# A transformer stack on one core: one maximum unit moved ahead of each score step, and another order of preparation in the 32-wide self-attention

## The reference

```python
x = x + _L0_xattn_ref(_layernorm(x), ctx_512, ...)   # causal self-attention + attention to the context, 16 heads of 8
x = x + _L0_ffn_ref(...)
x = x + _L1_xattn_ref(_layernorm(x), ctx_512, ...)   # attention to the context, 16 heads of 8
x = x + _L1_ffn_ref(...)
x = x + _L2_xattn_ref(_layernorm(x), ctx_512, ...)   # 16 heads of 32: self-attention (mask after softmax), MLP, then context, MLP
x = x + _L2_ffn_ref(...)
x = x + _L3_xattn_ref(_layernorm(x), ctx_512, ...)   # attention to the context, 16 heads of 8
x = x + _L3_ffn_ref(...)

# inside _L2_xattn_ref, the first _mha
a = softmax(einsum('bhsd,bhtd->bhst', q, k) * D ** (-0.5))
a = a * (t <= s)
o = einsum('bhst,bhtd->bhsd', a, v)
```

## Time and profile before

| what | value |
|---|---|
| median of 3 runs | 8038.86 us (8022.59 to 8043.93) |
| the profiled execution | 8022.59 us, its span 8020.8 us |
| PE busy | 7135.1 us, 89% |
| DVE busy | 5918.4 us, 74% |
| ACT busy | 4951.6 us, 62% |
| POOL busy | 2313.2 us, 29% |
| TensorE clock granted, mean | 0.94 of full speed |

### The profile page before, as it was taken

How to read it: one execution, slowest core, us unless ns; L and a number is a source line. 1 busy time by engine, 2 the same in 40 slices (tenths; PEclk the granted TensorE clock), 3 DMA queues, 4 the chain that set the end, 5 groups by cost and what they waited for, 6 DMA issues and landing times. The chain is left out here.

```text
span 8020.8 us, 186125 instructions
## 1 busy us (share of the span) xinstructions
PE 7135.1 (89%) x73814; PEld 3142.3 (39%) x73814; DVE 5918.4 (74%) x12885; ACT 4951.6 (62%) x9846; POOL 2313.2 (29%) x2368
## 2 busy tenths in 40 slices
PE   6999999878999997888599999999998779999979
PEld 2333333353333333444244444444444533333335
DVE  6888888657989996677466666666665469899855
ACT  4778887636888884444255555555554248888852
POOL 1222222111121110444245444544444211221200
PEclk9999999888999998788699999999999779999989
DMA  4444333114433421000100000000000144434400
GB/s 97 101 95 92 83 83 92 45 26 100 99 89 77 99 65 31 15 16 13 53 6 8 7 6 10 6 10 6 7 3 18 49 83 96 96 84 85 97 22 14
DMA packets 319828, 417.80 MB, mean 52 GB/s; under 512 B 56533, under 2 KB 238053, under 8 KB 318968
## 3 DMA queue, kind: packets, MB, share of 16 engines
q1 hardware_dynamic: 317432, 405.36, 22.4%
q10 hardware_dynamic: 1536, 0.53, 0.0%
HBM read 225.41 MB, written 174.66 MB: 50 GB/s over the span
## 5 line engine op out<-in xcount | busy, mean ns | idle before, releaser
L687 ACT ACTIVATE a_probs<-scores_ps 128x512 f32<-128x512 f32 (+2 forms) x5248 | 2821.7, 591 | 356.2 <-PE scores_ps L607 263.4
L746 DVE TENSOR_REDUCE a_unit_max<-bank 128x1 f32<-128x512 f32 x3072 | 2004.0, 684 | 182.0 <-PE bank L594 147.3
L624 PE MATMUL bank<-a_probs,a_v_sb 128*9 128x256 f32 (+1 forms) x20992 | 1614.1, 379 | 29.4 <-ACT a_out_sb L694 20.4
L1275 ACT ACTIVATE cross_probs<-scores_ps 128x512 f32<-128x512 f32 (+1 forms) x1792 | 869.4, 571 | 772.6 <-PE scores_ps L1172 772.6
L1357 DVE TENSOR_REDUCE cross_unit_max<-bank 128x1 f32<-128x512 f32 x1536 | 1006.5, 687 | 319.7 <-PE bank L1158 316.9
L607 PE MATMUL scores_ps<-a_stack 64*128 64x256 bf16 (+1 forms) x10496 | 1131.5, 275 | 61.6 <-ACT a_probs L687 55.8
L1441 POOL TENSOR_TENSOR cross_added<-cross_probs 128x1024 f32<-128x1024 f32 x384 | 902.4, 2350 | 944.6 <-PE bank L1205 868.8
L746 DVE TENSOR_REDUCE a_unit_max<-scores_ps 128x1 f32<-128x512 f32 x1536 | 1050.2, 684 | 162.1 <-PE scores_ps L594 144.6
L594 PE MATMUL bank<-a_stack 63*128 63x512 bf16 (+2 forms) x3413 | 1039.7, 372 | 8.1 <-DMA a_stack<-a_stack_dram 2.6
L607 PEld LDWEIGHTS scores_ps<-a_stack 64*128 64x128 bf16 (+1 forms) x10496 | 373.5, 96 | 991.9 <-ACT a_probs L687 832.8
L594 PE MATMUL scores_ps<-a_stack 63*128 63x512 bf16 (+2 forms) x1707 | 635.9, 373 | 50.8 <-DMA a_stack<-a_stack_dram 47.5
(11 more groups left out here) (421 smaller groups left out, 10119.5 us busy)
## 6 DMA issues: line engine op xcount, KB each, us to landing
a_stack_dram<-a_parts SPq DMA_DIRECT2D x288, 400.2 KB, 4.3
a_stack<-a_stack_dram SPq DMA_DIRECT2D x256, 348.2 KB, 8.0
a_stack<-a_stack_dram SPq DMA_DIRECT2D x128, 444.2 KB, 9.9
a_ctxT<-in_ctxT SPq DMA_DIRECT2D x48, 400.2 KB, 4.9
a_stack_dram<-a_parts SPq DMA_DIRECT2D x288, 64.0 KB, 2.7
a_stack_dram<-a_parts SPq DMA_DIRECT2D x96, 128.0 KB, 2.8
f_x<-x_after_dram SPq DMA_DIRECT2D x32, 256.0 KB, 3.6
x_after_dram<-a_res SPq DMA_DIRECT2D x48, 128.0 KB, 4.6
```

Source lines behind the costliest of these rows:

```text
L624: ins = pe.matmul(out_bank[32 * h:32 * h + V8, q0:TOK], v[0:n, e.t, 4 * e.g + h, :], A.probs[0:n, held, o + q0:o + TOK], start=(e.t == 0), ...
L687: act.activation(by_pair(A.probs[0:n, b, a * 512:(a + 1) * 512])[:, :, q0:TOK], by_pair(score_bank[(2 * e.i + a) % 3][0:n, :])[:, :, q0:TO ...
L746: ins = dve.tensor_reduce(unit_max[:, e.g % 2, qt, 2 * a + j, c:c + 1], bank[:, 0:e.s.chunks[c][1]], AX.X, ALU.max)
L1275: act.activation(probs[0:n, b, h, 0:m, :].rearrange("p m q -> p (m q)"), score_bank[h][0:n, 0:m * TOK], ACT.Exp, scale=scale).then_inc(S[" ...
```

## The change

In `segment8` the first unit of each step now stands before the step's scores instead of behind them; the second stays where it was. In `segment32`, for the self-attention only, the layer norms, the turned input and the first two `qk` and the first quad's units are made earlier in the list (for the batch after the next one), each `turn` belongs to the next batch, and the values move to steps 2 and 3. Third, DVE copies the values out of their bank instead of ACT.

```diff
@@ segment8
         units = units_at.get(n, [])
+        plan += units[0:1]
         if with_core and n < end:
             plan.append(Ev("scores", s=steps[n][0], g=steps[n][1], t=steps[n][2], i=cur * end + n))
-        plan += units[0:2]
+        plan += units[1:2]
         i = n - LAG8
@@ segment32
     if s.own:
         if with_ahead:
-            for i, kind in enumerate(("ln1", "ln2", "ln3", "ln4")):
-                put(i, 2, kind)
-        prepare(1, 1, True, "x_turned")
+            for i, slot, kind in ((0, 0, "ln1"), (0, 1, "ln2"), (1, 0, "ln3"), (1, 2, "ln4"), (2, 0, "x_turned"), (2, 2, "qk")):
+                put(i, slot, kind)
+            for k in range(s.NU):
+                units_at.setdefault(3, []).append(Ev("unit", k=k, r=int(k == s.NU - 1)))
+            put(3, 2, "qk", g=1)
         for g in range(QUADS):
-            step, late = (g + 1) % QUADS, g == QUADS - 1
-            prepare(step, 2, not late, "qk", g=g)
-            step, late = (g + 2) % QUADS, g >= QUADS - 2
-            for k in range(s.NU):
-                prepare(step, 0, not late, "unit", g=g, k=k, r=int(k == s.NU - 1))
-            prepare((g + 3) % QUADS, 0, g == 0, "turn", g=g)
-        prepare(3, 1, True, "v", j=0)
-        prepare(0, 1, False, "v", j=1)
+            if g >= 2:
+                prepare(g - 2, 2, True, "qk", g=g)
+            for k in range(s.NU * (g > 0)):
+                prepare(g - 1, 0, True, "unit", g=g, k=k, r=int(k == s.NU - 1))
+            prepare(g, 0, True, "turn", g=g)
+        prepare(2, 1, True, "v", j=0)
+        prepare(3, 1, True, "v", j=1)
         proj_at = (2, 1)
@@ segment32, the batch of an event
-        if e.kind in AHEAD32 and not (s.own and e.kind == "x_turned"):
+        if e.kind in AHEAD32 or s.own and e.kind in ("qk", "unit") and not e.nxt:
             e.batch = cur + 2
@@ program_act: "v" of the self-attention is no longer its work
-                if e.kind in SIDE32 and e.kind != "proj" and not (own and e.kind == "turn"):
+                if e.kind in SIDE32 and e.kind != "proj" and not (own and e.kind in ("turn", "v")):
...
-                    if e.kind == "v" and own:
-                        ins = act.activation(v_sb[:, m, e.j, :], side_bank[:, :], ACT.Copy)
@@ program_dve
+                if e.kind == "v" and own:
+                    dve.wait_ge(S["side_ps"], e.n + 1)
+                    dve.tensor_copy(v_sb[:, p, e.j, :], side_bank[:, :]).then_inc(S["side_done"], 1)
```

More of the change, by code:

```diff
@@ L1302, in program_act @@
                         ins = act.activation(k_tiles(e, 0), side_bank[:, 0:n].rearrange("p (j n) -> p j n", n=P), ACT.Copy)
-                    if e.kind == "v" and own:
-                        ins = act.activation(v_sb[:, m, e.j, :], side_bank[:, :], ACT.Copy)
-                    if e.kind == "v" and not own:
+                    if e.kind == "v":
                         n = s.tiles[2 * e.j][1]
```

## The result

| kernel | median | range of runs |
|---|---|---|
| before | 8032.98 us (4 runs) | 8022.59 to 8043.93 |
| changed | 8227.05 us (4 runs) | 8218.04 to 8235.57 |

The ratio is 1.0242 [1.0222, 1.0261]: slower by some 194 us. The direction was forecast, and 8227 lies inside the range of 7960 to 8270, but the forecast was 8122 (its sum adds 96 us to the profiled execution of before), and its own range ended at 8190. What has to be explained is a rise twice as large as foreseen.

What follows compares the result with a forecast made beforehand. Attention was taken as paced by DVE (about 1.2 us a plain step) or ACT's loop (1.14), own by its step's chain; 8022.6 us + 48 (attention) + 48 (own) = 8119, stated as 8122, range 7960 to 8270 us.

Steps and rivals of the forecast that it cites:

- term of the stage own: Stage own: +2.0 us of chain and +1.0 us of clock a batch, 16 batches, +48 us, between -20 and +80.
- `turn` behind `x_turned`: Own, step 2: `turn` must wait for ACT's two copies behind the four exponentials, +2.0 us a batch.
- `proj` behind `v`: Own: `proj` stands behind a `v` and waits for its copy, now DVE's, +0.85 us a batch.
- `x_turned` and `ln2` leave, `ln2` before the reciprocal: Own: `x_turned` leaves step 1's chain, `ln2` its place before a `turn` copy, perhaps delaying the reciprocal 0.2: -0.85 us a batch.
- clock (PE busy): Own: about 3 us of idle PE in step 2 may lower the clock; a third of 3.1 us, +1.0 a batch.
- The attention term: Stages a0, a1, a3: the even unit ahead of the scores costs +1.0 us a batch, 48 batches, +48 us.
- behind four `turn`s and four `quad_out`s: Attention: ACT already waits there, so the next exponential starts 0.22 us later; half of 1.7 us counted, +0.8 a batch.
- DVE's earlier unit: Attention: DVE gets the even unit about 0.22 us earlier, -0.5 us a batch of at most -1.3.
- The faster one: Rival: the even unit fills PE's waits and feeds DVE earlier, -62 us, own +0: 7960 us; 22%.
- Nothing to be seen: Rival: attention gains and loses alike, own loses less than thought, within 24 us of before, 8000 to 8046; 18%.
- ACT's loop shows everywhere: Rival: DVE does not pace, plain steps take 1.225 us, full-array side jobs cost 0.21; attention +211, 8282 us; 12%.
- Strict order across the row halves: Rival: PE keeps program order, units no longer run in pairs, 7.7 us a batch, +370 us, with own 8440 us; 5%.

Runs made afterwards that it cites:

- e6: Changed kernel with segment8 as before, plus the first `v` of a batch moved to step 1 in own: 8109.57 us, ratio 1.0081 to before.
- e8: Changed kernel with segment8 as before, plus `ln2` at the end of step 0 and `ln3` in slot 1 of step 1: 8108.14 us, ratio 1.0081.
- e7: Changed kernel with segment8 as before, GpSimd adding one head of four in own, the other sums left out: 8113.33 us, ratio 1.0091.
- e5: Changed kernel with segment8 as before, plus `turn` put ahead of `x_turned` in step 2 of own: 8093.09 us, ratio 1.0061.
- e3: Kernel before with the segment8 edit alone and even units on rows 64 to 127, odd on 0 to 63: 8032.35 us, ratio 0.9996.
- e4: Kernel before with only the rows of the units swapped, both units still behind the scores: 8048.62 us, ratio 1.0011.
- e1: Kernel before with the segment8 edit alone: 8127.69 us, ratio 1.0114.
- e11: Changed kernel with segment8 as before, plus 16 unused small matmuls ahead of every `turn`'s wait in own: 8137.59 us, ratio 1.0145.
- e9: Changed kernel with segment8 as before, plus the edits of e5, e6 and e8 together: 8064.39 us, ratio 1.0051.
- e12: e3 plus 16 unused small matmuls ahead of every `turn`'s wait in own: 7998.93 us against 8025.1 before, ratio 0.9971.

## Why the prediction was right or wrong

**The step that failed is the term of the stage own**, "+3.0 us a batch, 16 batches: +48 us". It measured +115, outside its own bounds of -20 to +80. By its own parts, per batch over the ten batches:

| part | forecast | measured |
|---|---|---|
| `turn` behind `x_turned` | +2.0 | +1.9 |
| `proj` behind `v` | +0.85 | +0.78 |
| `x_turned` and `ln2` leave, `ln2` before the reciprocal; `ln3` and copy of `v` at 0 | -0.85 | +1.5 |
| PE idle, sum | +2.0 | +4.2 (6.0 to 10.2) |
| clock (PE busy) | +1.0 | +3.6 (29.5 to 33.1) |
| batch | +3.0 | +7.85 (35.5 to 43.3) |

The +1.9 is how much later `turn` starts behind the first exponential, the +0.78 a wait; the +1.5 is what the sum of idle time leaves beside the two. Counted as waits alone, PE's in the ten batches of before and of the changed kernel are, for each batch: `turn` for ACT's line 1321 0 and 2.5 us, `turn` for maxima 3.4 and 4.1, units 2.3 and 2.65, `proj` 0 and 0.78.

Three things went wrong.
- *The clock was sized at a third of its bound.* The bound, 3.1 us between a batch at 0.90 and one at 0.77, was itself too small. The same trace of before has batches, from one `x_turned` to the next, that lie further apart:

```profile
3433.40:3471.60 38.20, 33.98 (x303) 18.23 (x302) 26.33 (x58) 17.20 (x32) 17.00 (x19) 0.73 0.05 15
```

```profile
3680.40:3713.10 32.70, 25.25 (x303) 14.13 (x302) 26.09 (x58) 17.10 (x32) 16.98 (x19) 1.00 0.05 14
```

  They differ by 5.5 us in length and by 8.7 us of PE's busy time, for the same 303 matmuls. The low level, half of full speed, covers 22.5 us of a batch in the record of the clock now and 10.2 before. e6 and e8 show directly that here an edit worth little or nothing in idle time moves the stage by 33 us.
- *"`ln3` stays before a `turn` copy: 0."* It stayed before the copy, but in a step in which GpSimd's addition is still under way. What was checked was DVE's order, not what runs on GpSimd beside it. e7 shows this cause. That `ln2`, now before the reciprocal, was foreseen to cost 0.2 and costs more is only read in the trace: the `turn` behind it waits 2.31 us for its maximum, where 1.18 is usual. e8 moves both norms at once and does not part them.
- *The run-in was not in the sum.* An order that prepares two batches ahead has 24 us more to do before the first exponential, and the last batch gives 9 us back. "+3.0 us a batch, 16 batches" has no such term. The batches themselves, +6.7 us in each of the other 15, are still the larger part of the miss.

The parts hold one against another as well: the `turn` wait (e5) alone makes half of the loss, and its mechanism, place and size of 1.9 us are as forecast.

**The attention term, +48, measured +75.** The mechanism stood: e3 takes it away with the order untouched. Per step in a1 (from one exponential to the next, medians) plain steps alternate between 1.15 and 1.30 us, mean 1.22, as worked out; the mean was already 1.19 before. Steps behind a `turn` went from 1.41 to 1.62 and those behind a `quad_out` from 1.49 to 1.68, the forecast's 0.2 us. A batch is 1.5 us longer (74.36 to 75.86), not 1.0. Its 52 steps, each averaged over the 16 batches of a1 and sorted by the job in front of it, give:

| steps of a batch in a1 | forecast | measured |
|---|---|---|
| plain (22 were counted, 29 have no job) | +0.7 | +0.7 (34.5 to 35.2) |
| behind four `turn`s and four `quad_out`s | +0.8 | +1.3 (13.0 to 14.3) |
| DVE's earlier unit; measured: the 12 steps with keys or values alone | -0.5 | -0.5 (21.55 to 21.05) |

So one size was off. The side jobs were counted half, "in the half of the batch that DVE paces", and came nearly whole: three of the four `turn`s cost 0.2 us each, one 0.02. The gain of 0.5 us came, but in the steps of keys and values, and not as shorter waits of DVE for units, which grew. e3, where the even unit is just as early, has it as well (-0.8 against e4); what makes it is not shown.

**The rivals.** The faster one is refuted by e1 and by DVE's waits; its "+0" for own also left out the 32 us of waits that the prediction itself counts there. "Nothing to be seen" fell with the result. "ACT's loop shows everywhere" asked for 4.4 us a batch where 1.5 came: of the 1.9 us of it that plain steps were to cost, 0.7 came. Strict order across the row halves is refuted by the rows at 7271.46 and by e3: two kernels with one order on PE that differ by 1.0114 to 0.9996.

**The sum.** 8022.6 + 96 is 8119; with the 16 us by which the median lay above the profiled execution it would have been 8135, not 8122. That slip of 13 us changes nothing in what was missed.

**Left open.** How much of own's 115 us the clock would give back with all waits as they are, since e11's fillers stood in the chain; the share of `ln2`; which edit of e9 makes the waits that are left in its batches; whether a shorter run-in can be had with this order; and why own differs by up to 18 us between profiles with the same code in it.

## What to carry to other kernels

Where two row tiles of PE feed one consumer in turn, put the filler on the tile that is consumed second: the same move in the order cost 1.1% on one half and nothing on the other. Price a new wait of PE in a stage whose clock already falls at its own length and the clock's share behind it, which here nearly doubled it (4.2 us of idling and 3.6 us of slower matmuls a batch). An order that prepares further ahead pays at its start: count that once. Before a DVE instruction is moved, look at what GpSimd does at its new place. A side job whose copy-out stands behind long work of ACT belongs behind the critical side job that shares its bank, not before it.

## What the runs showed of the hardware that was not expected

- A DVE instruction of 128x128 fp32 with its operands in SBUF took up to 1581 ns beside GpSimd's addition of 128x1024 (2.35 to 2.52 us), against 349 ns at most beside a smaller one (e7). In e8 the same kind of instruction took 1562 ns at most beside the addition and 661 ns at least beside GpSimd's masking of 128x512 (line 1438).
- Sixteen small matmuls per step raised the granted clock in ten batches of own from 0.86 in before to 0.94 (e12), and in the changed order from 0.74 to 0.83 (e11). Only the first was worth time.
- Two orders can idle alike and be granted different clocks: e8 idles 108.9 us of 409.5 at 0.81, the changed kernel 102.3 of 433.4 at 0.74.
